# Constants in one array, gate weights spread in four pieces, and a new order of all steps in a two-layer MetaFormer kernel

## What is computed

```
x = x + L0_conv(ln(x))    # projection, a 128x16 state per image, layer norm over 128, projection back
t = t + L0_ffn(ln(t))     # 8 experts, hidden 128, all computed, weighted by a top-2 gate
x = x + L1_conv(ln(x))    # 3x3 neighbourhood of squares plus a channel mix, x * (.)^-0.5
t = t + L1_ffn(ln(t))     # 8 experts, hidden 256, all computed, weighted by a top-2 gate
# an expert layer: out = sum over e of w[:, e] * (gelu(t @ W1[e] + b1[e]) @ W2[e] + b2[e])
```

## Time and profile before

| | |
|---|---|
| median of 3 runs | 713.8 us (709.12 to 715.76) |
| the profiled execution | 720.69 us, its span 718.7 us |
| busy in the span | PE 540.9, DVE 498.3, ACT 384.7, POOL 283.9 us |
| mean granted TensorE clock | 0.915 of full |

### The profile page before, as it was taken

How to read it: one execution, slowest core, us unless ns; L and a number is a source line. 1 busy time by engine, 2 the same in 40 slices (tenths; PEclk the granted TensorE clock), 3 DMA queues, 4 the chain that set the end, 5 groups by cost and what they waited for, 6 DMA issues and landing times.

```text
span 718.7 us, 10356 instructions
## 1 busy us (share of the span) xinstructions
PE 540.9 (75%) x3906; PEld 267.2 (37%) x3906; DVE 498.3 (69%) x831; ACT 384.7 (54%) x456; POOL 283.9 (40%) x241
## 2 busy tenths in 40 slices
PE   2314674688788979799779888897889786975867
PEld 1213233333333534354335433453345332421423
DVE  3266267868797968887988698788978795356312
ACT  2112712566577556756585558565866573543532
POOL 2122146134534553535452553365345332334013
PEclk9999975699999998989999989899999999989688
DMA  4500600063206130505041502450145005500230
GB/s 67 95 10 1 133 1 1 2 133 81 39 1 135 43 78 16 121 17 118 16 101 37 117 16 50 85 120 16 27 94 118 17 19 102 119 15 0 49 78 22
DMA packets 27840, 41.49 MB, mean 58 GB/s; under 512 B 11792, under 2 KB 19088, under 8 KB 27792
## 3 DMA queue, kind: packets, MB, share of 16 engines
q1 hardware_dynamic: 27152, 38.75, 26.5%
q0 software_dynamic: 640, 2.10, 1.0%
HBM read 38.22 MB, written 2.62 MB: 57 GB/s over the span
## 4 chain that ended last, share of the span: by engine, by line
DVE 27%; PE 24%; DMA 23%; issue 7%; POOL 7%; ACT 7%; SPq 5%; POOLq 0%; DVEq 0%; ACTq 0%
DMA WB<-w_scratch 19%; PE hP L857 8%; PE yP L873 7%; DMA w_scratch<-wTs 3%; SPq L408 3%; PE sA L772 2%; POOL stat_c L494 2%; ACT H L703 2%; DVE xsplit L985 2%; PE sA L782 2%; DVE xnrm L978 1%; DVE xnrm L973 1%; POOL stat_d L494 1%; DVE gt L1004 1%; DVE xcen_b L978 1%
## 5 line engine op out<-in xcount | busy, mean ns | idle before, releaser
L703 ACT ACTIVATE H<-hP,b 128x1024 f32<-128x1024 f32 x192 | 210.2, 1112 | 95.0 <-PE hP L857 93.2
L873 PE MATMUL yP<-H,w 128*64 128x512 f32 x768 | 205.5, 618 | 25.2 <-DVE ACC L1194 24.7
L857 PE MATMUL hP<-xT,w 128*64 128x512 f16 x1536 | 214.2, 403 | 3.0 <-ACT H L703 2.9
L563 POOL TENSOR_TENSOR ACC<-ACC,YW 128x512 f32<-128x512 f32 x96 | 128.8, 1347 | 201.4 <-DVE YW L1194 201.4
L857 PEld LDWEIGHTS hP<-xT,w 128*64 128x64 f16 x1536 | 83.4, 115 | 127.1 <-issue 74.2
L1194 DVE SCALAR_TENSOR_TENSOR YW<-yP,b,WB 128x512 f32<-128x512 f32 x96 | 71.5, 745 | 30.3 <-PE yP L873 29.9
L873 PEld LDWEIGHTS yP<-H,w 128*64 128x64 f32 x768 | 54.1, 142 | 68.4 <-issue 40.1
L1194 DVE SCALAR_TENSOR_TENSOR ACC<-yP,b,WB 128x512 f32<-128x512 f32 x32 | 23.1, 746 | 58.9 <-DMA WB<-w_scratch 58.9
L1150 DVE SCALAR_TENSOR_TENSOR nacc<-PAD,taps,nacc 128x528 f32<-128x528 f32 x56 | 49.2, 879 | 1.7
L886 PEld LDWEIGHTS sC<-fold,ACC 128*128 128x128 f32 x256 | 33.1, 202 | 31.3 <-issue 24.9
L886 PE MATMUL sC<-fold,ACC 128*128 128x64 f32 x256 | 37.6, 293 | 7.1 <-POOL ACC L563 6.4
(11 more groups left out here) (145 smaller groups left out, 752.7 us busy)
## 6 DMA issues: line engine op xcount, KB each, us to landing
WB<-w_scratch SPq DMA_DIRECT2D x32, 1024.0 KB, 10.3
X<-in_x SPq DMA_DIRECT2D x8, 256.0 KB, 12.0
out<-X POOLq DMA_DIRECT2D x8, 256.0 KB, 2.8
H<-in_L_ffn_W SPq DMA_DIRECT2D x2, 512.0 KB, 6.3
H<-in_L_ffn_W SPq DMA_DIRECT2D x2, 256.0 KB, 4.2
w<-in_L_ffn_W SPq DMA_DIRECT2D x1, 512.0 KB, 4.9
w_scratch<-wTs SPq DMA_DIRECT2D x16, 32.0 KB, 1.8
w<-in_L_ffn_W SPq DMA_DIRECT2D x1, 256.0 KB, 4.2
```

Of the source, the lines that this page charges most:

```text
L563: pool.tensor_tensor(ACC[l][:, cols], ACC[l][:, cols], YW[:, u % 4, :], ALU.add).then_inc(summed, 1)
L703: nc.scalar.activation(H[:, s % RING, :], hP[s % 2][:, :], ACT.Gelu, bias=b1[l][:, e * ch + c:e * ch + c + 1], scale=1.0 / WS)\
L857: mm = nc.tensor.matmul(hP[s % 2][b * C:(b + 1) * C, hf * HALF:(hf + 1) * HALF], w1[l][:, sp, w, b * C:(b + 1) * C], xT[l][g % 2][:, hf * ...
L873: mm = nc.tensor.matmul(yP[hf][a * C:(a + 1) * C, :], w2[l][:, (2 * j + a) * ch + c, :], H[:, (2 * ch * j + 2 * c + a) % RING, hf * HALF:( ...
```

## The change

1. On the host all constants are laid out as one array `consts`, W1 and W2 of both layers in the layout of their tiles. The kernel loads them in six transfers; the tokens of groups 0 and 1 are the first and third transfer of the queue. `mix` comes complete, so it needs no memset.
2. The staged W1 lie in `WB[1]`, no longer in `H`. `prepare("experts0")` comes behind `prepare("in")`, `prepare("experts1")` behind the gate weights of group 0. PE waits for them before the first chunk.
3. The tokens of group g+1 (from 2 on) are fetched over a slot table in which `decay` of SP stands 33.5 slots earlier.
4. `WB` is filled by eight transfers, two (64 partitions x 4 KB) for each pair j, with a semaphore for each j; DVE waits for the pair that it needs. A piece may start once the group before has used this pair.
5. All tables are new, in half slots. On PE the W2 product of a slot (`second`) now stands half a slot behind the W1 product, so that a step can stand between them.

```diff
 PE_AT = dict(
-    ab=dict(turn_a=12, proj0=17, proj1=19, proj2=20, c_cols=21, state=23, y0=24, y1=26, turn_hi=32,
-            turn_lo=34, mix_out=35, turn_b=38, gate=41, send=43),
-    cd=dict(turn_c=4, pool0=4, turn_u=11, turn_d=15, gate=16, send=19),
-    final=(12, 14, 24, 26))
+    ab=dict(turn_a=14.5, proj0=17, proj1=18, proj2=20.5, c_cols=23.5, state=25, y0=26, y1=27.5, turn_hi=33,
+            turn_lo=33.5, mix_out=34, turn_b=39.5, gate=40, send=43.5),
+    cd=dict(turn_c=2.5, pool0=3.5, turn_u=10, turn_d=16, gate=17, send=20.5),
+    final=(12.5, 12.5, 21.5, 24))
 DVE_AT = dict(
-    ab=dict(centre_a=0, sums_a=6, norm_a=10, decay=21, values=22, y0=25, y1=27, centre_n=28, sums_n=29,
-            norm_n=30, mix_out=35, centre_b=35, sums_b=36, norm_b=37, top2=41, weights=41),
-    cd=dict(centre_c=1, sums_c=1, norm_c=3, pool0=5, pool1=6, pool2=7, pool3=7, turn_u=10, centre_d=10,
-            sums_d=12, norm_d=14, top2=17, weights=18),
-    final=(12, 13, 24, 27))
+    ab=dict(centre_a=-3, sums_a=6, norm_a=8.5, decay=21.5, values=23, y0=26.5, y1=28.5, centre_n=29, sums_n=30.5,
+            norm_n=31.5, mix_out=34, centre_b=35, sums_b=36, norm_b=38.5, top2=40, weights=40.5),
+    cd=dict(centre_c=-1, sums_c=0.5, norm_c=2, pool0=5.5, pool1=5.5, pool2=7.5, pool3=7.5, turn_u=10, centre_d=10.5,
+            sums_d=12, norm_d=14, top2=16.5, weights=19.5),
+    final=(12.5, 13, 20.5, 25.5))
...
 SP_AT = dict(
-    ab=dict(decay=22, send=41),
-    cd=dict(send=21),
+    ab=dict(decay=-11.5, send=20.5),
+    cd=dict(send=-5),
...
-            load("in", both_halves(win_f, W_in) + [(dtb[:, :], rep(dt_bias)), (alog[:, :], rep(A_log))])
...
-                    sp.dma_start(mix[r:r + 8, r:r + 8], gk[:, grp * 8:grp * 8 + 8]).then_inc(mix_loaded, 16)
...
+            sp.dma_start(K[:, 0:n_first], consts[:, 0:n_first]).then_inc(loaded["first"], 16)
+            sp.dma_start(tiled(X0[1]), grouped(xd, 1)).then_inc(x_loaded[1], 16)
+            sp.dma_start(w1_f[0], m0_W1).then_inc(loaded["w1_0"], 16)
+            sp.dma_start(K[:, n_first:], consts[:, n_first:]).then_inc(loaded["rest"], 16)
+            sp.dma_start(w2[0][:, :, :].rearrange("p n f -> p (n f)"), m0_W2).then_inc(loaded["w2_0"], 16)
+            sp.dma_start(w1_f[1], m1_W1).then_inc(loaded["w1_1"], 16)
+            sp.dma_start(w2[1][:, :, :].rearrange("p n f -> p (n f)"), m1_W2).then_inc(loaded["w2_1"], 16)
...
                 sp.dma_start(scratch[l][i].rearrange("e (t p) -> (e t) p", p=P), wTs[l][:, :]).then_inc(w_out[l][i], 16)
-                sp.wait_ge(w_out[l][i], 16 * (g // 2 + 1))
+
+            def spread_piece(l, g, j):
+
+                sp.wait_ge(w_out[l][g % 2], 16 * (g // 2 + 1))
                 if g >= 1:
-                    sp.wait_ge(scaled, 8 * (POS[(l, g - 1)] + 1))
+                    sp.wait_ge(scaled, 8 * POS[(l, g - 1)] + 2 * j + 2)
+                elif l == 1:
+                    sp.wait_ge(prep, PREP["experts1"])
                 for a in range(2):
-                    src = scratch[l][i].rearrange("(j a) n -> a j n", a=2)[a]
-                    sp.dma_start(WB[l][a * C:a * C + C, :, :], src.partition_broadcast(C)).then_inc(w_in[l][i], 16)
+                    sp.dma_start(WB[l][a * C:a * C + C, j, :],
+                                 scratch[l][g % 2][2 * j + a:2 * j + a + 1, :].partition_broadcast(C)
+                                 .rearrange("c a n -> c (a n)")).then_inc(w_in[l][j], 16)
...
                     if g == 0:
                         prepare("in")
+                        prepare("experts0")
...
                     gate_weights(0, g)
+                    if g == 0:
+                        prepare("experts1")
...
-                    if j == 0 and hf == 0:
-                        dve.wait_ge(w_in[l][g % 2], 32 * (g // 2 + 1))
+                    if hf == 0:
+                        dve.wait_ge(w_in[l][j], 32 * (g + 1))
```

More of the change, by code:

```diff
@@ L99, in final_slots, with walk @@
     return m + at["final"][2 * layer], m + at["final"][2 * layer + 1]
-def walk(moe, final, ab, cd, at, store=None):
-    for slot in range(ab_start(0), moe_start(1, GROUPS - 1) + 2 * SLOTS):
+def walk(moe, final, ab, cd, at, store=None, second=None):
+    for half_slot in range(2 * (moe_start(0, 0) - 3 * SLOTS), 2 * (moe_start(1, GROUPS - 1) + 3 * SLOTS)):
+        slot = half_slot / 2
         for g in range(GROUPS):
@@ L108, in walk @@
                 if 0 <= s < E * CHUNKS[layer] + LAG + 2:
-                    moe((layer, g), s)
+                    if s == int(s):
+                        moe((layer, g), int(s))
+                    elif second:
+                        second((layer, g), int(s))
         for g in range(GROUPS):
@@ L114, in walk @@
                         final((layer, g), half)
+        for g in range(GROUPS):
             if store and slot == moe_start(1, g) + STORE_AT:
@@ L120, in walk, with build_metaformer @@
                         stage(g, step)
[L123 to L129, removed]
+LOADS = {"first": 1, "rest": 1, "w1_0": 1, "w2_0": 1, "w1_1": 1, "w2_1": 1}
+FIRST = dict(win_f=PROJ, dtb=HEADS, alog=HEADS, dpar=HEADS, wout_f=C, gam_col=1, bet_col=1)
+REST = dict(gw_f0=E, gb0=E, b1_0=E * CHUNKS[0], b2_0=PAIRS, gw_f1=E, gb1=E, b1_1=E * CHUNKS[1], b2_1=PAIRS, taps=9,
+            nbias=1, go_col=1, bo_rep=C, mix=P)
+PREP = {"in": 3, "experts0": 7, "out": 11, "bias": 12, "experts1": 17}
+def build_metaformer(nc, x, consts, m0_W1, m1_W1, m0_W2, m1_W2, out):
     ORDER = sorted(((l, g) for l in range(2) for g in range(GROUPS)), key=lambda m: moe_start(*m))
@@ L167, in build_metaformer @@
         out_bias = sb("out_bias", [P, C])
-        dtb = sb("dtb", [P, HEADS])
-        alog = sb("alog", [P, HEADS])
         expa = sb("expa", [P, HEADS])
-        dpar = sb("dpar", [P, HEADS])
-        gw_f = [sb(f"gw_f{l}", [P, E]) for l in range(2)]
         gw = [sb(f"gw{l}", [P, 2, E], F16) for l in range(2)]
-        gb = [sb(f"gb{l}", [P, E]) for l in range(2)]
+        K = sb("K", [P, sum(FIRST.values()) + sum(REST.values())])
+        col = {}
+        at = 0
+        for name, width in list(FIRST.items()) + list(REST.items()):
+            col[name] = K[:, at:at + width]
+            at += width
+        win_f, dtb, alog, dpar, wout_f = (col[n] for n in ("win_f", "dtb", "alog", "dpar", "wout_f"))
+        gam_col, bet_col, taps, nbias = (col[n] for n in ("gam_col", "bet_col", "taps", "nbias"))
+        go_col, bo_rep, mix = (col[n] for n in ("go_col", "bo_rep", "mix"))
+        gw_f, gb, b1, b2 = ([col[f"{n}{l}"] for l in range(2)] for n in ("gw_f", "gb", "b1_", "b2_"))
         NC = [E * c for c in CHUNKS]
@@ L318, in sums_until @@
             return 6 * (u // 8) + max(0, u % 8 - 1)
-        A_USES = ("turn_a", "proj0", "proj1", "proj2", "c_cols", "state", "y0", "y1", "turn_hi", "turn_lo", "mix_out",
-                  "turn_b", "gate", "send")
-        C_USES = dict(turn_c="turn_c", pool="pool0", turn_u="turn_u", turn_d="turn_d", gate="gate", send="send")
+        C_USES = dict(turn_c="turn_c", pool0="pool", turn_u="turn_u", turn_d="turn_d", gate="gate", send="send")
         def previous(uses):
[L327 to L333, removed]
+            return dict(zip(uses[1:], uses))
+        a_order, c_order = [], []
+        walk(lambda m, s: None, lambda m, half: c_order.append((("fin", m[0], half), m[1])),
+             lambda g, k: a_order.append((k, g)), lambda g, k: c_order.append((C_USES[k], g)), PE_AT)
+        BEFORE_A = previous(a_order)
+        BEFORE_C = previous(c_order)
         def a_read(name, g):
@@ L412, in _ @@
[L412 to L419, removed]
@@ L429, in _ @@
[L429 to L436, removed]
+            n_first = sum(FIRST.values())
@@ L457, in ab @@
                     spread_weights(0, g)
+                    for j in range(PAIRS):
+                        spread_piece(0, g, j)
             def cd(g, k):
@@ L461, in cd @@
                     spread_weights(1, g)
+                    for j in range(PAIRS):
+                        spread_piece(1, g, j)
             def moe(m, s):
@@ L693, in moe @@
                     if n == 0:
-                        act.wait_ge(prep, PREP["experts1"])
-                        act.wait_ge(loaded["experts0"], 16 * LOADS["experts0"])
-                    elif m == (1, 0) and s == 0:
-                        act.wait_ge(loaded["experts1"], 16 * LOADS["experts1"])
+                        act.wait_ge(loaded["rest"], 16)
                     if n >= RING:
@@ L1095, in ab @@
                     square_sum("n", g)
-                    if g == 0:
-                        prepare("experts0")
                 elif k == "norm_n":
@@ L1118, in ab @@
                 elif k == "top2":
-                    if g == 0:
-                        prepare("experts1")
                     top2(0, g, sA)
@@ L1224 @@
     arrays, args = {}, []
-    for name in _INS:
-        a = np.ascontiguousarray(inputs[name])
```

(3 more changed lines are left out.)

142 lines of the change are left out of this document (72 added, 70 removed).

## The result

The changed kernel takes 623.4 us (median of 4, 623.1 to 628.5) against 713.7 before: ratio 0.874, 95% interval 0.870 to 0.879.

What follows compares the result with a forecast made beforehand. It took the loop through the weight-spreading transfer (19% of the span) as the bound. Terms 7.9 + 0.8 + 7.0 + 25 + 5.5 + 6.5 = 52.7 us off 720.7 gave 668.0, as a median 662; range 634 to 692.

Steps and rivals of the forecast that it cites:

- the loop through `WB`: Spreading gate weights holds DVE, behind whose queued work the next gate product waits; DVE stood 58.9 us in sixteen waits.
- the pieces: Weight spreading in four pairs: first piece there about 5.5 us after the write instead of 13; the first layer's 7.0 go.
- The new order: Steady periods: later sends take back 1.5 and 4.7 us, tighter PE handoffs cost 2 us a period, bounds 0 and 4.
- three quarters: Of 33.2 us in the remaining thirteen waits for `WB`, 25 us come home, giving a period of about 70.5 us.
- the start: First `y0` addition no longer waits for group 1's tokens, 7.9 us; `prepare("experts1")` no longer ahead of `top2`, 0.8 us.
- eighth group: DVE's wait for `WB` at the third-last expert layer goes: 5.54 us.
- last layer: DVE's 13.20 us wait for `WB` at the last expert layer shrinks to about 5; gain 6.5 us.
- Rival D: The first piece lands no sooner than 10 us while `cd` is sent 1.5 slots later: 742 us; chance 0.04.
- Rival A: Steady periods tighten to some 66.5 us, PE's busy time and little more: 24 us beyond the forecast, 638; chance 0.20.
- the transfer's share of the chain: Sign in the changed profile: the `WB` transfer's share of the chain under 8%, where it was 19% of the span.
- Meetings of DVE and POOL: DVE operations slowed beside POOL's adds, 11 us a period, are shuffled by the order; no change taken, bounds 3 us either way.
- The rival's "above 630": Expectation for one 512 KB transfer over 128 partitions per piece: over 1 us slower or faster, 615 to 619 or above 630.

Runs made afterwards that it cites:

- old order: The changed kernel with the old PE, ACT, DVE and POOL tables and W2 right behind W1; 655.9 us with four pieces, 697.7 us with whole transfers.
- the constants' kernel: The changed kernel with the old tables, W2 right behind W1 and two whole weight transfers, keeping packed constants, early tokens and moved preparations: 697.7 us (0.979).

## Why the prediction was wrong

The direction and the loop through `WB` were right, and the pieces gave nearly what the sum says. The step that failed is the last of its working, "The new order": it lists what the new order costs and has no term for what it gives ("So of 33.2 us I let three quarters come home"). A second term, the start, was too small.

| term of the sum | forecast | measured |
|---|---|---|
| start (tokens, preparations), with the rest of the constants' part | 8.7 | 15 |
| pieces: first layer 7.0, eighth group 5.5, last layer 6.5, three quarters of the others 25 | 44 | 42, in the old order |
| the new order | 0 | 33, with the pieces |

- **The pieces.** The price of 4.2 to 5.5 us for the first pair held: 4.9 us in the median, 4.6 at the last layer. In the old order with pieces the forecast had said 662 us and 655.9 were measured. The page of the Trainium skill that spoke against small transfers (DMA: Bandwidth & Descriptors) had no say. The estimate worked out from its formula, which is a fit for transfers that GpSimd issues, was 21 us for eight small transfers in a row against 9 for two large ones; the trace shows 11.7 against 12.7, the pieces landing some 1.1 us apart behind the first at 3.7. No wait stood at a later piece. Rival D is refuted.
- **The start.** `y0` came 9.6 us sooner where 7.9 were counted. ACT's squares of the tokens, which stood behind its first use of a constant, began 0.9 us sooner (SP's queue ahead of that constant had been set at nothing), and PE's `y0` product took 1.12 us where it took 2.04, which no term had; why isn't shown. In the constants' kernel the weights left 11.9 us sooner. In the changed kernel the new order takes 3.4 us of this back, and the 8.4 us that are left agree with the 8.7 of the sum by luck.
- **The new order.** The forecast listed the handoffs that become tighter and found them, rightly, small: PE's wait for POOL at the folds is 15.0 us in all, some 2 us a group. It did not list those that become looser. With the wait for `WB` gone, PE in the old order stood 8.6 us a period, and the forecast had no row for that: the windows showed only how far PE and DVE were from their floors. The new order took about half of it away, at `xsplit`, `xg` and `Vs` (42.5 us in all in the old order, 5.4 in the new one). Rival A had this mechanism and even its size (a period of 66.5; 66.3 measured), at 0.20. It came to 638 and not 623 mostly since it took over the forecast's terms for the end, 5.5 and 6.5 us, where 14.3 and 10.2 went (the last two parts of the table of spans), and the range ended at 634.
- **The signs that it named.** `y0` by 31 us, the waits for `WB` below 15 us in total with none in the middle, the first piece under 6 us, and the transfer's share of the chain came as said. The periods did not (66 and not 69 to 72), nor the last wait for `WB` (8.1 us and not about 5).
- **Meetings of DVE and POOL.** They were shuffled, as said. DVE's busy time sank by 11 us in all between the old order with pieces (494.5) and the new one (483.0). Three groups, in the old order and then in the new one:

```profile
L960 DVE TENSOR_TENSOR Yc<-Yc,stat_n 128x1024 f32<-128x1024 f32 x8 | 17.1, 2144 | 4.1 <-POOL stat_n L476 4.1
...
L1006 DVE TENSOR_TENSOR gt<-gt 128x64 f32<-128x64 f32 x16 | 10.4, 649 | 0.6
...
L960 DVE TENSOR_TENSOR xcen<-xcen,stat_a 128x512 f32<-128x512 f32 x8 | 5.5, 686 | 6.2 <-POOL stat_a L476 6.2
```

```profile
L960 DVE TENSOR_TENSOR xcen<-xcen,stat_a 128x512 f32<-128x512 f32 x8 | 16.4, 2055 | 3.9 <-POOL stat_a L476 3.9
...
L960 DVE TENSOR_TENSOR Yc<-Yc,stat_n 128x1024 f32<-128x1024 f32 x8 | 9.7, 1218 | 2.1 <-POOL stat_n L476 2.1
...
L1006 DVE TENSOR_TENSOR gt<-gt 128x64 f32<-128x64 f32 x16 | 4.5, 284 | 0.6
```

  In the old order seven of the eight `Yc` overlap one of POOL's sums into `ACC` and take 2.3 us each; in the new one they overlap none and take 1.2, also where a small `stat` operation of POOL runs beside them. The gate's chain of small operations meets POOL less (33 and 42 of its 160 in the new and the old order). `xcen` of stage a took meetings over, with POOL's `ysplit` in seven of eight. That the total alone doesn't set the time is shown by POOL's old table: less DVE time, 46 us slower. That the exchange itself carries a share of the 33 us is not shown.

What stays open is how the 33 us divide over the steps. The experiments show that the tables fit each other and the pieces, and that neither of the parts tried, the folds and POOL's table, gives anything alone in the old order.

## What to carry to other kernels

Where engines run queues in a fixed order, price a new order together with the shortened transfer: an order that sends the weights later was a loss of 32 us with a transfer of 13 us, and a gain of 33 us with one of 5 us. When a wait on the path is removed, the new floor is the busiest engine, and a schedule that was rebuilt as a whole may come near it (PE 94% busy in a period); give that case more than a rival's chance. Undoing one part of such an order measures how well it fits, not what it is worth; put parts forward too.

## What the runs showed of the hardware

Here one transfer whose source are two rows of DRAM, each spread over 64 partitions, was far slower than two transfers of one row each, with the same bytes. SP's own rows in that kernel; then windows of it while such transfers run (length, busy us of PE, PEld, DVE, ACT and POOL, the clock, the DMA share, GB/s):

```profile
240.27 0.50 SPq L415 DMA_DIRECT2D w_scratch<-wTs  x1
242.08 18.68 SPq L424 DMA_DIRECT2D WB<-w_scratch  x4
```

```profile
312.00:316.00 4.00, 4.00 (x33) 1.61 (x30) 3.93 (x6) 3.10 (x4) 1.75 (x2) 1.00 0.13 53
...
320.00:324.00 4.00, 3.76 (x34) 2.05 (x30) 3.69 (x10) 3.93 (x7) 1.96 (x2) 1.00 0.13 52
```

Four issues took 18.7 us where eight took 4.9, and while they ran the DMA share was 0.13 of sixteen engines, which is two of them: it seems that the transfer was divided over its outer dimension of two. At 53 GB/s the 2 MB of a layer need some 40 us by an estimate, where the eight transfers had landed after 11.7, and the kernel took 839 us. The rival's "above 630" holds, by far more than it meant. Whoever merges broadcasts should look at the DMA share of the window first.
